# Third norm's statistics and token numbers on ScalarE; the last ranks inside the down product; first expert loads and products in another order

## What is computed

```python
xn = norm(x)                                  # first norm, then an affine one
q, k, v = xn @ wq + bq, xn @ wk + bk, xn @ wv + bv
fq, fk = elu(q) + 1, elu(k) + 1
attn = fq @ (fk^T v) / (fq . sum(fk) + 1e-6)  # per token, over its 16 heads of 16
a = xn0 + attn @ wo + bo                      # xn0: the layer's normed input
x1 = x + a + gelu(norm2(a) @ fc_w + fc_b) @ proj_w + proj_b
r = norm(x1)                                  # third norm, no weights
logits = r @ gate_w.T;  w, e = softmax(top_2(logits))
shared = (silu(r @ sg_gate.T) * (r @ sg_up.T)) @ sg_down.T
routed = sum over the token's 2 experts of w * ((silu(r @ wg[e].T) * (r @ wu[e].T)) @ w_down[e].T)
out = x1 + shared + routed
```

## Time and profile before

| | |
|---|---|
| median of 3 timed runs | 1788.8 us (1788.29 to 1788.81) |
| the profiled execution | 1787.39 us, span 1785.3 us |
| TensorE busy | 1662.2 us, 93% |
| VectorE busy | 1212.4 us, 68% |
| GpSimd busy | 1190.9 us, 67% |
| ScalarE busy | 805.2 us, 45% |
| granted TensorE clock | 0.977 of full, mean |

### The profile page before, as it was taken

How to read it: one execution, slowest core, us unless ns; L and a number is a source line. 1 busy time by engine, 2 the same in 40 slices (tenths; PEclk the granted TensorE clock), 3 DMA queues, 4 the chain that set the end, 5 groups by cost and what they waited for, 6 DMA issues and landing times.

```text
span 1785.3 us, 25208 instructions
## 1 busy us (share of the span) xinstructions
PE 1662.2 (93%) x7115; PEld 1203.4 (67%) x7161; DVE 1212.4 (68%) x2117; ACT 805.2 (45%) x1837; POOL 1190.9 (67%) x668
## 2 busy tenths in 40 slices
PE   2588999999999999999999998989999999999997
PEld 1354665665665665566566565668888888888886
DVE  7999999999999999999999996132222222222221
ACT  4255556556565465465465454323232323223232
POOL 4978889899898898898898893224333333433333
PEclk8798999999999999999999999989999999999999
DMA  5102112111111112112112112066777767777774
GB/s 201 47 13 71 48 40 57 48 34 50 59 29 53 56 27 59 47 35 59 48 35 60 48 25 60 25 188 158 156 166 154 169 152 166 157 157 164 155 169 77
DMA packets 89455, 157.19 MB, mean 88 GB/s; under 512 B 8896, under 2 KB 72128, under 8 KB 89024
## 3 DMA queue, kind: packets, MB, share of 16 engines
q1 hardware_dynamic: 60512, 112.58, 20.4%
q0 software_dynamic: 28896, 44.06, 14.6%
HBM read 101.79 MB, written 48.56 MB: 84 GB/s over the span
## 4 chain that ended last, share of the span: by engine, by line
PE 56%; DVE 20%; POOL 12%; issue 8%; ACT 3%; DMA 1%; POOLq 0%; SPq 0%; DVEq 0%; ACTq 0%
PE p_b L1502 10%; PE p_b L1513 10%; PE p_q L1502 7%; PE p_b L1332 7%; PE p_b L1379 6%; PE p_b L1445 5%; DVE p_q L931 5%; POOL prod_pool L496 4%; DVE prod L922 4%; DVE prod L945 4%; PE p_v L1502 3%; POOL prod_pool L510 2%; DVE qkv L958 2%; PE p_q L1304 2%; POOL prod_pool L517 2%
## 5 line engine op out<-in xcount | busy, mean ns | idle before, releaser
L611 POOL DMA_INDIRECT out_rows<-prod_pool,prod x142 | 220.7, 1554 | 383.6 <-ACT prod_pool L849 353.3
L496 POOL TENSOR_TENSOR prod_pool<-prod_pool 128x2048 f32<-128x2048 f32 (+2 forms) x192 | 370.7, 1931 | 15.1
L1379 PE MATMUL p_b<-bT,fc_sb 128*128 128x512 f32 x512 | 230.4, 604 | 1.3 <-ACT bT L781 1.3
L1332 PE MATMUL p_b<-proj_sb,hid 128*128 128x256 f32 x1024 | 230.5, 379 | 0.0
L1332 PEld LDWEIGHTS p_b<-proj_sb,hid 128*128 128x128 f32 x1024 | 189.6, 190 | 29.4 <-issue 0.5
L931 DVE TENSOR_REDUCE p_q<-prod 128x128 f32<-128x2048 f32 (+1 forms) x64 | 189.3, 2957 | 1.2
L922 DVE TENSOR_TENSOR prod<-p_q,eqk 128x4096 f32<-128x4096 f32 (+1 forms) x48 | 186.8, 3891 | 4.8 <-DVE attn L971 0.3
L945 DVE TENSOR_TENSOR prod<-p_q,v_dve 128x4096 f32<-128x4096 f32 (+1 forms) x48 | 186.8, 3891 | 1.6
L958 DVE TENSOR_REDUCE qkv<-prod 128x256 f32<-128x4096 f32 (+1 forms) x48 | 186.6, 3887 | 1.6
L1502 PE MATMUL p_b<-prod,exp_up 128*128 128x256 f32 x840 | 187.1, 379 | 0.0
L1445 PE MATMUL p_b<-x3T,sgup_sb 128*128 128x512 f32 x384 | 177.5, 601 | 6.4 <-issue 5.5
(11 more groups left out here) (179 smaller groups left out, 2880.7 us busy)
## 6 DMA issues: line engine op xcount, KB each, us to landing
exp_up<-in_experts SPq DMA_DIRECT2D x71, 768.0 KB
prod<-rows_sorted SPq DMA_DIRECT2D x71, 260.0 KB
xin<-in_x SPq DMA_DIRECT2D x16, 512.0 KB, 3.4
xres<-in_x SPq DMA_DIRECT2D x16, 512.0 KB, 3.7
xres<-xmid POOLq DMA_DIRECT2D x16, 512.0 KB, 4.6
out_rows<-x SPq DMA_DIRECT2D x16, 512.0 KB, 2.9
exp_dn<-in_experts SPq DMA_DIRECT2D x8, 384.0 KB, 5.1
out_rows<-prod_pool,prod POOLq DMA_INDIRECT x142, 3.8
```

The costliest lines, as they stand in the source:

```text
L496: done(g.tensor_tensor(prod_pool[:, at:at + n * w], prod_pool[:, at:at + n * w], prod_pool[:, at + n * w:at + 2 * n * w], ALU.add))
L611: pool.indirect_dma_start(out=out[:, :], out_offset=bass.IndirectOffsetOnAxis(ap=tok_i[j][:, a:a + 1], axis=0), in_=yg[j][:, a * D:(a + 1) ...
L1332: ins = t_.matmul(o, src[:, k, t * P:(t + 1) * P], w[:, k, :], start=k == 0, stop=bias_at is None and k == chunks - 1)
L1379: ins = t_.matmul(bnk[:], fc_sb[:, k, f * P:(f + 1) * P], bT[:, k, :], start=k == 0, stop=k == KC - 1)
```

## The change

1. The third norm's statistics go from VectorE to ScalarE. `residual_2` is left with its add, and each half announces `x1_read` by itself. `shift_3` and `scales_3` go. `ln3_scales(c, j, k)` does for two tiles at a time: sums by a copy that accumulates, the mean, sums of squares, `Ln`, `Exp`, and the product with the mean. Both halves stand between `take_qkv(c + 1, 0)` and `take_qkv(c + 1, 1)`. What waited for `x1_read` waits for the half or the two halves that it needs.
2. The token numbers are moved on and copied by ScalarE (`token_numbers`, ahead of the second norm's `bT`), and GpSimd's `scatter` waits for them.
3. In period 17 `ranks` stands after two of the four tiles of `down`, and not after all four.
4. SP waits for the tables and loads the up weights of the first two expert tiles before it stores the pads; the rows of both tiles follow the pads. TensorE does `gate_up(0, 0)` before `gT(1, 1)`.
5. `gate_last` works by thirds, each as soon as its up product is taken.

```diff
 ORDER = (POOL_TILE, 0, 1, 2)
-POOL_STEPS = 16
+POOL_STEPS = 14
 HH = HEADS * HD
...
-                    wait(sp, x1_read, c - 1)
+                    wait(sp, x1_read, 2 * (c - 1))
                     sp.dma_start(xres[:], x_blk[bass.ds(c - 1, 1)].rearrange("b p t d -> p (b t) d")
...
+            def load(k, j):
+                row = sp.value_load(tab_row[0:1, bass.ds(k, 1)], min_val=0,
+                                    max_val=EXPERTS * REGION + (SPARE_TILES - 1) * TILE)
+                wait(sp, gT_psum, k - 1)
+                wait(sp, xg_meta, k - 1)
+                sp.dma_start(xg[j], rows_sorted[bass.ds(row, TILE), :].rearrange("(a p) r -> p a r", p=P)
+                             ).then_inc(xg_loaded[j], 16)
+            def load_up(k, j):
+                e = sp.value_load(tab_ei[0:1, bass.ds(k, 1)], min_val=0, max_val=EXPERTS - 1)
+                wait(sp, gu_psum, HCH * (k - 1))
+                sp.dma_start(exp_up[j][:], experts[bass.ds(e, 1), :, 0:EXU].rearrange("a p n -> p (a n)")
+                             ).then_inc(up_loaded[j], 16)
+            sp.wait_ge(tables_ready, 1)
+            load_up(0, 0)
+            load_up(1, 1)
             sp.wait_ge(pads_at, 1)
...
-            sp.wait_ge(tables_ready, 1)
             sp.wait_ge(pads_stored, 16 * EXPERTS)
             sp.wait_ge(scattered, 16 * 2 * TPB * BLOCKS)
-            def load(k, j):
...
-            def load_up(k, j):
...
             load(0, 0)
-            load_up(0, 0)
             load(1, 1)
-            load_up(1, 1)
             store(BLOCKS + 1, BLOCKS + 1)
...
+                wait(pool, tok_written, c - 1)
                 wait(pool, slots_ready, c - 1)
-                stand_alone(pool)
-                done(g.tensor_scalar(tok[:], tok[:], float(BLOCK), None, ALU.add))
-                stand_alone(pool)
-                done(g.tensor_copy(rows[j % 2][:, :, C_TOK], tok[:]))
                 stand_alone(pool)
...
-            def scales_3(c):
-                wait(act, x1_read, c)
-                a.activation(sq_c[:], mv_c[:, :, 1], ACT.Ln, bias=eps_1[:, 0:1]).then_inc(ln3_log, 1)
-                act.wait_ge(ln3_log, c)
+            def ln3_scales(c, j, k):
+                tiles = range(TPB // 2 * k, TPB // 2 * (k + 1))
+                half, n = slice(tiles[0], tiles[-1] + 1), 2 * (c - 1) + k + 1
+                wait(act, x1_read, n)
+                for t in tiles:
+                    a.activation(act_junk[:, t, :], x1[(j + 1) % 2][:, t, :], ACT.Copy, accum_out=sum_c[:, t:t + 1]
+                                 ).then_inc(ln3_sum, 1)
+                act.wait_ge(ln3_sum, TPB // 2 * n)
+                a.activation(mean_c[:, half], sum_c[:, half], ACT.Copy, scale=-1.0 / D).then_inc(ln3_mean, 1)
+                act.wait_ge(ln3_mean, n)
+                for t in tiles:
+                    a.activation(act_junk[:, t, :], x1[(j + 1) % 2][:, t, :], ACT.Square, bias=mean_c[:, t:t + 1],
+                                 accum_out=square_c[:, t:t + 1]).then_inc(ln3_var, 1)
+                act.wait_ge(ln3_var, TPB // 2 * n)
+                a.activation(sq_c[:, half], square_c[:, half], ACT.Ln, bias=eps_1[:, 0:1], scale=1.0 / D
+                             ).then_inc(ln3_log, 1)
+                act.wait_ge(ln3_log, n)
                 wait(act, rows_ready, TPB * (c - 1))
-                a.activation(rs_c[:, 0, :], sq_c[:], ACT.Exp, scale=-0.5).then_inc(ln3_std, 1)
+                a.activation(rs_c[:, 0, half], sq_c[:, half], ACT.Exp, scale=-0.5).then_inc(ln3_std, 1)
+                act.wait_ge(ln3_std, n)
+                for t in tiles:
+                    a.activation(rs_c[:, 1, t:t + 1], rs_c[:, 0, t:t + 1], ACT.Copy, scale=mean_c[:, t:t + 1]
+                                 ).then_inc(ln3_scale, 1)
...
-                wait(act, ln3_scale, n)
+                wait(act, ln3_scale, TPB * n)
                 if isinstance(n, int) and n == 1:
...
                 norm(lambda t: rows[j % 2][:, t, 0:D], lambda t: x1[j % 2][:, t, :], rs_c, rows_ready)
+            def token_numbers(c, j):
+                a.activation(tok[:], tok[:], ACT.Identity, bias=block_1[:, 0:1]).then_inc(tok_moved, 1)
+                act.wait_ge(tok_moved, c - 1)
+                a.activation(rows[j % 2][:, :, C_TOK], tok[:], ACT.Copy).then_inc(tok_written, 1)
...
                     keep_scales(c)
+                if stage_c:
+                    token_numbers(c, j)
                 if more and not stage_b:
...
                     take_qkv(c + 1, 0)
+                if stage_b:
+                    ln3_scales(c, j, 0)
+                    ln3_scales(c, j, 1)
+                if more:
                     take_qkv(c + 1, 1)
-                if stage_b:
-                    scales_3(c)
                 if stage_c:
...
                 wait(dve, proj_psum, 2 * (c - 1) + k + 1)
-                done(v.tensor_tensor(flat[:, 512 * k:512 * k + 512],
-                                     res[:, 512 * k:512 * k + 512], (p_b0, p_b1)[k][:], ALU.add))
-                for t in range(TPB // 2 * k, TPB // 2 * (k + 1)):
-                    done.later(v.bn_stats(st6[:, t, :], x1_b[:, t, :]))
-                if k == 1:
-                    averages(mv_c)
-                    dve.sem_inc(x1_read, 1)
-            def shift_3(c):
-                wait(dve, ln3_std, c)
-                done(v.tensor_copy(shift_c, mv_c[:, :, 0]))
-                v.scalar_tensor_tensor(rs_c[:, 1, :], shift_c, -1.0, rs_c[:, 0, :], ALU.mult, ALU.mult
-                                       ).then_inc(ln3_scale, 1)
+                v.tensor_tensor(flat[:, 512 * k:512 * k + 512], res[:, 512 * k:512 * k + 512], (p_b0, p_b1)[k][:],
+                                ALU.add).then_inc(x1_read, 1)
...
                     inverse(den_0[:, 0:2 * HEADS + POOL_HEADS])
-                if stage_b:
-                    shift_3(c)
                 if core:
...
                     if more:
-                        if stage_b:
-                            dve.wait_ge(ln3_scale, c)
                         dve.sem_inc(pq_free, 1)
...
             done(v.memset(eps_1[:], EPS))
+            done(v.memset(block_1[:], float(BLOCK)))
             done(v.memset(eps_2[:], EPS * EPS))
...
             def gate_last():
-                wait(dve, up_taken, 2 * HCH * BLOCKS)
                 wait(dve, shared_h, BLOCKS - 1)
-                announce(dve, v.tensor_tensor(sg_g[:], sg_g[:], sg_u[:], ALU.mult), shared_h, BLOCKS)
+                for i in range(HCH):
+                    wait(dve, up_taken, 2 * HCH * (BLOCKS - 1) + 2 * (i + 1))
+                    ins = v.tensor_tensor(sg_g[:, i, :], sg_g[:, i, :], sg_u[:, i, :], ALU.mult)
+                    if i < HCH - 1:
+                        done.later(ins)
+                    else:
+                        done.sync()
+                        announce(dve, ins, shared_h, BLOCKS)
...
                     wait(pe, attn_ready, c)
-                    wait(pe, x1_read, c - 1)
+                    wait(pe, x1_read, 2 * (c - 1))
                     wait(pe, up_taken, 2 * HCH * (c - 3) + 3)
...
                 if stage_d:
-                    down(c, range(TPB - 1 if stage_b else TPB))
+                    down(c, range(TPB - 1 if stage_b else TPB // 2 if stage_c else TPB))
+                if stage_c and not stage_b:
+                    ranks(c)
+                    down(c, range(TPB // 2, TPB))
                 if stage_b:
...
                             ranks(c)
-                elif stage_c:
-                    ranks(c)
                 if core:
...
                     if three and n == 2:
-                        wait(pe, x1_read, c)
+                        wait(pe, x1_read, 2 * c - 1)
                     if n >= 2:
...
             gT(0, 0)
+            gate_up(0, 0)
             gT(1, 1)
-            gate_up(0, 0)
             pe.wait_ge(out_ready, BLOCKS)
             def step(k, j):
```

More of the change, by code:

```diff
@@ L131, in build @@
         rs_b = sb("rs_b", [P, 2, TPB])
[L132 removed]
+        sum_c = sb("sum_c", [P, TPB])
+        mean_c = sb("mean_c", [P, TPB])
+        square_c = sb("square_c", [P, TPB])
         sq_c = sb("sq_c", [P, TPB])
@@ L268, in build @@
         xsum_ready = sem("xsum_ready")
+        ln3_sum = sem("ln3_sum")
+        ln3_mean = sem("ln3_mean")
+        ln3_var = sem("ln3_var")
         ln3_std = sem("ln3_std")
@@ L427, in _ @@
             periods(sp, body)
-            sp.wait_ge(pads_at, 1)
-            sp.wait_ge(init_stored, 48)
-            for e in range(EXPERTS):
-                row = sp.value_load(pad_at[0:1, e:e + 1], min_val=0, max_val=EXPERTS * REGION - TILE)
-                sp.dma_start(rows_sorted[bass.ds(row, TILE), :],
-                             rows_sorted[EXPERTS * REGION:EXPERTS * REGION + TILE, :]).then_inc(pads_stored, 16)
-            sp.wait_ge(tables_ready, 1)
-            sp.wait_ge(pads_stored, 16 * EXPERTS)
-            sp.wait_ge(scattered, 16 * 2 * TPB * BLOCKS)
             def load(k, j):
@@ L455, in load_up @@
```

(13 more changed lines are left out.)

5 lines of the change are left out of this document (3 added, 2 removed).

## The result

The changed kernel takes 1792.31 us (1789.45 to 1794.41), the kernel before, in the same rounds, 1787.17; the ratio is 1.0024, 95% interval 1.0018 to 1.0031. It is slower by a little over the 0.2% that can be told from nothing; the forecast was 1786.5, "the same". The profiled execution took 1791.53 us, its span is 1789.4 (before 1785.3), the granted clock 0.973 (before 0.977).

The account below looks back on a forecast made before the run. The period was VectorE's stretch (49.8 us) plus TensorE's (18.2), handed to one another. Terms -11.1 - 1.7 + 4.7 + 1.5 + 1.5 + 2.8 = -2.3 us gave a median of 1786.5 us, range 1780.5 to 1792.

Parts of the forecast that it names:

- The loop: Steady periods: VectorE's stretch loses two bn_stats, -0.79 us each; ScalarE's sg_g comes 0.36 us later, thirteen times, +4.7 us.
- The start: Up to the add of period 2: -2.5 us, with 1.7 of statistics and shift leaving TensorE's wait for attn.
- Period 15: TensorE's wait moves to the fourth shared group, for sg_g, with half clock behind it: +1.5 us.
- the third group, held back: Period 15 before the change: the third group's four matmuls run at half clock behind the x1_read wait; warm they take 1.7.
- Period 16: sg_g starts at 1146.0 instead of 1144.54, on the chain to the last down: +1.5 us.
- The ranks: Period 17: ranks behind 12 instead of 24 matmuls of down, so place and tables come 2.6 us earlier.
- The pads: Tail, SP's queue: pads issued behind tables and two weight loads, landing at 1185, 5 us late against 1180.0.
- gT(1, 1): Tail, TensorE: it stands in front of gT(2), 0.44 us, with ScalarE's copy exposed, 0.7 us.
- B: Rival: in the steady periods TensorE's wait for sg_g outgrows what pq_free gave back; up to 1794.8 us; chance 0.18.
- A: Rival: the ScalarE sequence takes 2.9 us instead of 3.3 and costs the period nothing; 1781.8 us; chance 0.20.
- C: Rival: in the tail the pads do not bind, first products start 4 us earlier; 1780.9 us; chance 0.05.
- The signs: Profile values expected after the change: period 67.6 us, pq_free about 0.8, TensorE hole 0.5, attn wait under 4.

Follow-up runs that it names:

- e15: The kernel before with ranks inside the down product as the only edit; 1784.14 us, 0.9982.
- e3: The changed kernel with SP's order alone altered: the pads stored ahead of the tables' wait and both weight loads; 1784.46 us, 0.9985.
- e7: e6 with SP's whole order as before the change, TensorE's order staying changed; 1779.11 us, 0.9952.
- e5: The changed kernel with the third norm's statistics of period 16 alone back on VectorE (bn_stats); 1785.92 us, 0.9989.
- e6: e5 with the pads stored ahead of the weight loads; 1779.17 us, 0.9957.
- e18: e7 with period 15's third shared group held until both halves of x1 are there, as before the change; 1780.98 us, 0.9963.
- e11: e7 with ranks behind all 24 matmuls of down again; 1787.43 us, 0.9997.
- e2: The kernel before with only parts 3, 4 and 5 of the change; 1791.89 us, 1.0028.
- e9: e7 with two unused squares more on ScalarE in the third norm's second half, periods 1 to 15; 1805.51 us, 1.0094.
- e14: e7 with one square more on ScalarE in the third norm's second half; 1790.86 us, 1.0016.
- e1: The kernel before with only part 1 of the change, the third norm's statistics on ScalarE; 1783.91 us, 0.9983.
- e17: e7 with the second half's statistics on VectorE, the shift read through PSUM and pq_free waiting for it; 1788.32 us, 1.0005.
- e10: e7 with the second half's two squares left out, so not the reference's computation; 1775.06 us, 0.9926.

## Why the prediction was wrong

The step that failed is the price of the new waits for `sg_g` in periods 15 and 16. They were put at +1.5 us each, +3.0 together; the changed kernel takes 130.9 us from the add of period 15 to `place`, e15, which has the early ranks and the old statistics, 124.8: 6.1 us. The waits themselves were nearly right. What the sum left out is the clock behind them. The loop was right, and three other terms (start, pads, `gT(1, 1)`) came out too low by 1.7, 1.1 and 0.4 us.

- **The loop** (-0.79 and +0.36, thirteen times). Right in mechanism. That -5.4 us meets -5.6 is partly luck: the quiet periods gained more than the 0.43 us forecast, 0.6, and two VectorE stalls took 1.3 us back. e3 and e7, which have none, gained 6.6 and 6.5 there. The bound of 0.1 us for a wait in the loop is not seen: the second half takes 3.25 us in the loop and 3.36 in period 15, which is written out.
- **The start** (-2.5). Mis-sized: -0.8. The 1.7 us of statistics in period 1 were gained, but the half-clock stretch ended at 103.1 and not 100.5, and took 1.3 back (half of 2.6, an estimate). In e5 it ended at 99.8, with the same code up to there. The kernels of this study with the changed statistics in these periods show -0.8 to -2.9 at that point, so this term has a spread of 2 us that no edit made.
- **Period 15** (+1.5). Direction right, +2.4 in the changed kernel: the twelve matmuls behind the wait took 8.29 us where the working had 7.07. In e3, e5, e6, e7 and e18 they took 6.8 to 7.1, as worked out, and the period grew by 1.0 to 1.3 only, but there the clock is low once more in period 16, 1.7 us for 18 matmuls of `down` (e3, then the changed kernel):

```profile
1099.09 5.82 PE L1353 MATMUL p_b<-sgdn_sb,sg_g 128*128 128x256 f32 x18
1101.51 4.13 PE L1353 MATMUL p_b<-sgdn_sb,sg_g 128*128 128x256 f32 x18
```

  So either way the term is 2.4 to 3.0. That the third group, held back, costs half clock was wrong: it fits into the wait (e18).
- **Period 16** (+1.5). This step failed most: 3.6 (+1.0 in the table, with the ranks' -2.6 taken out). `sg_g` starts 2.0 us later behind the add of period 16 than before, where 1.5 was forecast, and TensorE stands 2.05 us. That the clock falls behind it, in a stretch that had kept it, was not in the sum: the twelve matmuls take 7.11 us instead of 5.32. Undoing the statistics there is worth 3.6 to 4.1 us by the traces, 5.3 to 6.4 by the times.
- **The ranks** (-2.6). Right: 2.6 in e15 and e11.
- **The pads** (5 us late, products +4.2 behind the tables). Right in mechanism, 1.1 short: the first weight load was issued 1.8 us behind the tables' last instruction (1168.60 to 1170.41), which I had put at nothing, and it was 1.1 in e2. The issues took 9.76 us instead of 10.66 and gave 0.9 back. The reading "at most 4.4 us to land" was loose, the rows give 4.9 (1175.87 to 1180.78); in the changed kernel it is 3.4. This is the largest single loss: e3 takes back 7.8 us, 6.0 of them in this stretch.
- **gT(1, 1)** (+1.1). Measured +1.5 to the end.
- **The rivals.** B named the right engine and the wrong place: ScalarE does take VectorE's place, but in the last two periods, and not in the loop. A falls (e9, e14): the second half took 3.25 us, not 2.9. C falls: the pads were issued only 0.9 us faster, and TensorE waits 10.13 us for the rows behind them. The Trainium skill's rule for ScalarE (*ScalarE: Activation LUTs*, "Rules for kernel authors") names `relu`, `max`, `min`, `add` and `mul` for VectorE, and not copies, as the prediction has it. It does not decide this case: in the loop the dearer engine was the free one, e1 is 3.7 us faster than before; in period 16, where ScalarE is on the path, the statistics cost less on VectorE, as the rule would have it.
- **The signs.** Period 67.4 us (67.6), `pq_free` 0.86 a wait (0.8), TensorE's hole ahead of the fourth group 0.3 (0.5), the row load behind the pads and long behind the scatter: these held. The wait for `attn` in period 2 is 4.69 us and not under 4. The products start 8.8 us later than the loop's gain would put them (1191.35 against 1188.80 - 6.2), where the sign said 1 to 2, and the prediction's own terms add up to 4.6. No sign was set for the clock in periods 15 and 16, so none could show the loss there.

With hindsight the sum lacked one kind of term: where a wait grows from nothing to 2 us, what TensorE does behind it is dearer too. The rows of before showed it (matmuls at half clock behind a 5.48 us wait), and I used it in period 15 only.

## What to carry to other kernels

A change that pays in the loop must be looked at in the written-out periods at its ends, where other work no longer covers it; there the better version may be the old one (e5). A queue's order is priced by what stands last in it: move a transfer ahead only past those that nothing waits for. Price a new wait on a full TensorE with the matmuls behind it, at half clock too. And before a difference of 1 to 3 us in one stretch of one trace is called an effect, look how far that stretch differs between kernels with the same code there: here 2 us at the start, and over 3 between `place` and the first row load.

## What the runs showed of the hardware

- A 128x2 instruction on VectorE took 2.46 us in the mean when it copied from SBUF to SBUF, and 2.47 with two SBUF operands, ending with GpSimd's product in 14 of 15 cases. With one operand in PSUM both took at most 0.16. The Trainium skill says so (*SBUF — State Buffer*, "Who interferes with whom": a copy can take the ports that VectorE shares with GpSimd, two inputs in SBUF need them while GpSimd reads SBUF, and whoever comes second waits for the whole instruction), and the traces agree.
- A row block of 260 KB was used 5.7 us after its issue with two weight loads issued ahead of it (e3), 2.8 with none (e7). The ring order of *DMA: Bandwidth & Descriptors* in the Trainium skill fits that; it is not shown, as the pads, issued right ahead of the weights in e3, may have kept these back.
- VectorE at times stands 0.4 to 1.9 us ahead of the second residual add, and ScalarE 2.1 us in e17, with nothing that the profile names; how often VectorE does changes from kernel to kernel in code that was not edited (four times in e11, never in e7). What causes it stays open, and with it a part of the steep price of e9 and e14.
- TensorE fell to 1.2 GHz behind a wait of 1.9 us in an otherwise full period (e9) and behind 2.05 us in period 16 of the changed kernel, and stayed at 2.4 through waits of 0.3 (the steady period above, granted clock 1.00).
- The same eight pad copies of 260 KB took 9.8 us to issue when GpSimd's scatter was over (changed kernel), and 10.1 (e1) to 15.2 (e10) when the scatter ran beside them.
